# Straight blocks in two stages of a fused 4-layer network: the second routed feed-forward in one block with its routing three groups ahead, and the product-key experts in one block of sixteen steps

## What is computed

```
# second routed feed-forward: one of 8 experts for each batch row
xn = layernorm(h)                                  # [32, 113, 256]
e  = argmax(mean(xn, over the 113 tokens) @ Wr + br)    # one expert number for each row
h += relu(xn[row] @ W1[e] + b1[e]) @ W2[e] + b2[e]      # 256 -> 1024 -> 256

# product-key experts: 8 heads, 8 of 64 x 64 keys for each token and head
xn   = rmsnorm(layernorm(h)) * w
idx  = top 8 of the sums of two top-8 lists of similarities, for each head
h   += sum over the chosen experts of gelu(xn . down[idx]) * relu(score) * up[idx]
```

## Time and profile before

| | us |
|---|---|
| median of 3 runs (lowest to highest) | 6021.89 (6014.45 to 6035.73) |
| the profiled execution, its own time | 6037.05 |
| its span in the trace | 6035.3 |
| second routed feed-forward, first matmul to end of the last residual | 3553.32 to 3911.52 |
| product-key steps, first matmul of the first to last residual | 4631.91 to 6031.2 |

### The profile page before, as it was taken

The page is one execution under the profiler, slowest core; times in us unless marked ns, Lnnn a source line. Parts: engine busy times, 40 slices in busy tenths (PEclk is TensorE's granted clock), DMA queues, the critical chain, the costliest instruction groups (busy, mean ns, idle before and its releaser), DMA issues. The chain is left out here.

```text
span 6035.3 us, 64217 instructions
## 1 busy us (share of the span) xinstructions
PE 4920.7 (82%) x21148; PEld 3219.8 (53%) x21148; DVE 3587.9 (59%) x7080; ACT 2192.0 (36%) x4034; POOL 2261.7 (37%) x1366
## 2 busy tenths in 40 slices
PE   7988699368888878888688767857776999999999
PEld 4555377223333333333244437823335998989998
DVE  3664122269889889898742220055554876867776
ACT  3553011055555545656422232234441222222222
POOL 2442300469999989999700000000001212212211
PEclk8998899589999989899889878978887999999999
DMA  1003133212222222222200006600001000000000
GB/s 66 1 1 108 41 120 99 73 57 71 69 68 69 65 70 69 69 71 69 64 0 5 0 0 237 242 3 0 0 0 74 4 3 4 4 3 4 4 4 4
DMA packets 153762, 289.17 MB, mean 48 GB/s; under 512 B 24373, under 2 KB 135468, under 8 KB 144650
## 3 DMA queue, kind: packets, MB, share of 16 engines
q1 hardware_dynamic: 146426, 267.00, 13.6%
q0 software_dynamic: 6144, 14.04, 0.8%
q10 hardware_dynamic: 912, 4.63, 0.2%
HBM read 254.96 MB, written 33.42 MB: 48 GB/s over the span
## 5 line engine op out<-in xcount | busy, mean ns | idle before, releaser
L1496 PE MATMUL ssm_ps<-ssm_hc,net_ident 128*128 128x452 f32 x2048 | 957.1, 594 | 195.3 <-DVE ssm_hc L1729 111.0
L1659 POOL TENSOR_TENSOR ssm_dBu<-ssm_du,ssm_bc 128x904 f32<-128x904 f32 x512 | 1066.6, 2107 | 14.9 <-DMA ssm_bc<-ssm_rows 12.5
L1585 ACT ACTIVATE ssm_ps<-ssm_step,ssm_decay 128x448 f32<-128x448 f32 x1024 | 649.6, 638 | 665.6 <-DVE ssm_ps L1719 433.8
L1496 PEld LDWEIGHTS ssm_ps<-ssm_hc,net_ident 128*128 128x128 f32 x2048 | 390.4, 203 | 728.9 <-issue 343.1
L2925 POOL TENSOR_TENSOR peer_hot_cols<-peer_hot_cols,peer_codesT 128x512 f32<-128x512 f32 (+1 forms) x240 | 288.5, 1202 | 1159.2 <-DVE peer_hot_cols L2941 1159.2
L1719 DVE TENSOR_TENSOR_SCAN ssm_ps<-ssm_ps,ssm_dBu 128x452 f32<-128x452 f32 x512 | 565.2, 1104 | 128.1 <-ACT ssm_ps L1585 43.8
L1719 DVE TENSOR_TENSOR_SCAN ssm_hs<-ssm_ps,ssm_dBu 128x452 f32<-128x452 f32 x512 | 551.7, 1077 | 62.6 <-ACT ssm_ps L1585 35.8
L1668 POOL TENSOR_TENSOR ssm_hc<-ssm_hs,ssm_bc 128x904 f32<-128x904 f32 x256 | 539.5, 2107 | 74.8 <-DVE ssm_hs L1719 74.6
L2835 PE MATMUL peer_ps<-peer_xn,peer_down 128*128 128x226 f32 x2048 | 451.3, 366 | 24.2 <-issue 17.3
L2938 DVE TENSOR_TENSOR peer_hot_rows<-peer_ramp,peer_codesT 128x1024 f32<-128x1024 f32 (+1 forms) x240 | 284.5, 1186 | 280.0 <-PE peer_ps L2850 249.6
L2850 PEld LDWEIGHTS peer_ps<-peer_hot_cols,peer_hot_rows 128*128 128x128 f32 x3616 | 436.0, 192 | 23.8 <-DVE peer_hot_rows L2938 22.6
(11 more groups left out here) (422 smaller groups left out, 8304.1 us busy)
## 6 DMA issues: line engine op xcount, KB each, us to landing
ssm_bc<-ssm_rows SPq DMA_DIRECT2D x256, 452.0 KB, 3.6
ex_w<-in_l_ffn_w SPq DMA_DIRECT2D x66, 1024.0 KB, 9.4
moe_w_gu<-in_moe_gate_up SPq DMA_DIRECT2D x16, 704.0 KB
slots_in<-rt_zeros SPq DMA_DIRECT2D x17, 640.0 KB, 8.5
moe_rows_in<-slots_in SPq DMA_DIRECT2D x16, 512.0 KB
slots_out<-xp_rows_out SPq DMA_DIRECT2D x16, 512.0 KB
moe_w_dn<-in_moe_down SPq DMA_DIRECT2D x16, 384.0 KB
peer_down<-in_peer_down_t SPq DMA_DIRECT2D x1, 4096.0 KB, 16.4
```

The lines of the kernel that those rows point to most:

```text
L1496: nc.tensor.matmul(Y_BANK[j][:, 0:GT], c["ident"][:, :], hc[:, q % 2, j, :], start=False, stop=(n == S - 1))\
L1585: nc.scalar.activation(rows(dA(i % 2))[:, :, lo:lo + N - 1], rows(step[hf.d][:, j, :])[:, :, lo:lo + N - 1], ACT.Exp, scale=decay[hf.d][:, ...
L1659: nc.gpsimd.tensor_tensor(dBu[:, q % 2, j:j + 2, :], du[hf.d][:, j:j + 2, :], bc[:, q % RING, 0:1, :].to_broadcast([P, 2, GT]), ALU.mult). ...
```

## The change

**Second routed feed-forward.** Everything is one straight block without loops. The norm, the token mean and the router work on one group at a time. Three groups (`AHEAD`) are done first, one after the other; groups 3 to 7 are worked into the expert rows of groups 0 to 4: the mean matmul behind the up matmuls of the group's row 0, the second moment behind those of row 1, the scores behind those of row 3. The normed groups go to four buffers `xs` (`XB`) and the two ScalarE copies are gone. The expert numbers of each group go to DRAM and back by two DMAs of GpSimd's queue. SyncE fetches the expert of row r as soon as row r - 4 is finished. Both halves of the down product share one PSUM bank, and the residual starts when both are done. The semaphores are cleared by GpSimd, as after the first routed feed-forward.

**Product-key experts.** The loop, its three borders and the variant of the step's columns that is taken from registers are gone; all sixteen steps stand in one block.

The core of the diff:

```diff
+    WB = 4
+    XB = 4
+    AHEAD = 3
     with Stage(nc, "ex2") as st:
-        with Stage(nc, "rt2") as sr:
-            with nc.Fori(0, GROUPS // NW) as g:
...
-        with nc.Fori(0, GROUPS) as g:
-            with nc.Block(no_gpsimd_drain=True) as block:
...
-            st.clear()
+        with nc.Block() as block:
+            @block.sync
+            def _(sp):
+                sp.dma_start(w_r[:, :, :], wr.rearrange("(k p) e -> p k e", p=P)).then_inc(s["loaded"], 16)
+                sp.dma_start(b_r[:, :], br.to_broadcast([GB, E])).then_inc(s["loaded"], 16)
+                for r in range(B):
+                    i = r % WB
+                    sp.wait_ge(s["id_in"], 16 * (r // GB + 1))
+                    if r >= WB:
+                        sp.wait_ge(s["down_done"], r - WB + 1)
+                        sp.wait_ge(s["res_done"], DK * (r - WB + 1))
+                    e = nc.sync.value_load(ids[0:1, r:r + 1], min_val=0, max_val=E - 1)
...
+            @block.gpsimd
+            def _(pool):
+                for g in range(GROUPS):
+                    rows = slice(g * GB, (g + 1) * GB)
+                    pool.wait_ge(s["best_done"], g + 1)
+                    nc.gpsimd.dma_start(row_expert[rows, :], best[:, g % 2, 0:1]).then_inc(s["sent"], 16)
+                    pool.wait_ge(s["sent"], 16 * (g + 1))
+                    nc.gpsimd.dma_start(ids[0:1, rows], row_expert[rows, :].rearrange("b a -> a b")).then_inc(s["id_in"], 16)
+                pool.wait_ge(s["id_in"], 16 * GROUPS)
...
+                # TensorE
+                for g in range(AHEAD):
+                    mean(g)
+                    var(g)
+                    scores(g)
+                for r in range(B):
+                    g, i = r // GB + AHEAD, r % GB
+                    up(r)
+                    if g < GROUPS:
+                        if i == 0:
+                            mean(g)
+                        if i == 1:
+                            var(g)
+                        if i == 3:
+                            scores(g)
+                    down(r)
...
+                # ScalarE: squares(g) behind the relus of row 0, roots(g) behind those of row 1
+                # VectorE: centre(g) ahead of the residual of row 1, scale(g) ahead of row 2's,
+                #          choose(g) (bias, maximum, index) behind row 3's
...
+        st.clear(pool_dmas=True)
@@ peer
         LAG = 3
-        U = 4
...
-        with nc.Fori(0, STEPS // U - 1) as g:
-            steps([pair_at(g, k) for k in range(U)], [pair_at(g, k + 1) for k in range(U)], [pair_at(g, k + 2) for k in range(U)])
-        tail = range(STEPS - U, STEPS)
-        steps([pair_cols(g) for g in tail], [pair_cols(g + 1) if g + 1 < STEPS else None for g in tail],
-              [pair_cols(g + 2) if g + 2 < STEPS else None for g in tail])
+        after = lambda g: pair_cols(g) if g < STEPS else None
+        steps([pair_cols(g) for g in range(STEPS)], [after(g + 1) for g in range(STEPS)], [after(g + 2) for g in range(STEPS)])
```

More of the change, by code:

```diff
@@ L2010, in l2_ffn @@
     HB = HID // P
+    WB = 4
+    XB = 4
+    AHEAD = 3
     with Stage(nc, "ex2") as st:
         ps = [st.psum(f"ps{i}") for i in range(8)]
-        normed = st.sbuf("normed", [P, DK, T])
-        means = st.sbuf("means", [P, DK, B])
-        with Stage(nc, "rt2") as sr:
-            NW = 2
-            norms = [Norm(sr, ps[2 * i], ps[2 * i + 1], f"ln{i}") for i in range(NW)]
-            kept, summed = sr.sem("kept"), sr.sem("summed")
-            with nc.Fori(0, GROUPS // NW) as g:
-                with nc.Block(no_gpsimd_drain=True) as block:
[L2021 to L2087, removed]
@@ L2089, in l2_ffn @@
-        WB = GB
+        UP_BANK, DOWN_BANK, LN_BANK = ps[0:4], ps[4:6], ps[6:8]
         W1 = [st.sbuf(f"w1_{i}", [P, DK, HID]) for i in range(WB)]
@@ L2093, in l2_ffn @@
         B2 = [st.sbuf(f"b2_{i}", [P, DK]) for i in range(WB)]
-        ids = st.sbuf("ids", [1, B + 1], U32)
+        w_r = st.sbuf("w_r", [P, DK, E])
+        b_r = st.sbuf("b_r", [GB, E])
+        ids = st.sbuf("ids", [1, B], U32)
         hid = st.sbuf("hid", [P, 2, HB, N])
-        x_in = st.sbuf("x_in", [P, DK, GT])
-        id_in = st.sem("id_in")
-        landed = [st.sem(f"landed{i}") for i in range(WB)]
[L2099 to L2108, removed]
+        xs = st.sbuf("xs", [P, XB, DK, GT])
+        centred = st.sbuf("centred", [P, DK, GT])
+        square = st.sbuf("square", [P, DK, GT])
+        log_var = st.sbuf("log_var", [P, GT])
+        rstd = st.sbuf("rstd", [P, GT])
+        total = st.sbuf("total", [P, DK, GB])
+        means = st.sbuf("means", [P, DK, GB])
+        score = st.sbuf("score", [GB, E])
+        top = st.sbuf("top", [GB, 8])
+        best = st.sbuf("best", [GB, 2, 8], U32)
+        names = ("loaded", "mean_mm", "centre_done", "square_done", "var_mm", "log_done", "rstd_done", "x_done", "total_done",
+                 "mean_done", "score_mm", "score_done", "top_done", "best_done", "sent", "id_in",
+                 "up_done", "relu_done", "down_done", "res_done")
+        s = {x: st.sem(x) for x in names}
+        landed = [st.sem(f"landed{i}") for i in range(WB)]
         with nc.Block() as block:
```

195 lines of the change are left out of this document (133 added, 62 removed).

## The result

| us | before | changed |
|---|---|---|
| median of 4 runs (lowest to highest) | 6025.34 (6014.45 to 6035.73) | 5925.01 (5908.74 to 5927.84) |
| the profiled execution (its span) | 6037.05 (6035.3) | 5927.84 (5926.1) |

The ratio is 0.983, with an interval of 0.980 to 0.985: 100 us less. The two traces differ by 109.2 us. Read at the same places in both, that splits as follows.

The account below looks back on a forecast made before the run. TensorE was taken to bound both stages, with losses at block borders. Experts 69.1 us less plus product keys 32.6 less made 101.7; from the median 6021.9 that gave 5920 us, range 5898 to 5950.

Parts of the forecast that it names:

- Opening: Ahead of the experts: three groups one after the other, 39.8 us at the lower clock, 34.9 at the higher.
- The numbers' way: Expert opening: expert numbers through DRAM and back by 24.3 us at the latest, row 0 loaded by 34.7, hidden before 39.8.
- Rows: Expert stage: 32 rows at 7.14 us, 228.5; cold first row +2.0; five norms of 3.4 between rows, 17.2; stage 288.6.
- The end of the stage: Expert stage's border to the next stage: 1.4 us before; a GpSimd clear may add 0 to 2, taken as 0.5.
- Product keys: Product-key stage: three borders become inner steps, 33.4 us less; 0.8 lost to clock drops, leaving 32.6.
- The clock drops: Product-key inner steps: some take 1.66 us more after a wait for codes; 0.8 for three more steps, range 0 to 20.
- The range's own terms: Whole kernel: opening 34.9 to 44, first row 1 to 3, end 0 to 2, clock drops 0 to 20: 5907 to 5945.
- Weights bind: Rival, expert stage: fetches get only 248 GB/s, 8.5 us a row, 26 us more, 5946; chance 0.08.
- Fresh code binds: Rival, product keys and experts: straight code must be waited for, 52 us less gained, 5972; chance 0.07.
- Slower than before: Rival, expert stage: four-buffer ring with landings of 40 us, kernel ends at 6058; decides from landings of 35; chance 0.03.

Follow-up runs that it names:

- sorted version: Changed kernel with semaphore numbers sorted before clearing, so one range instruction clears neighbours: 5804.62 us, ratio 0.973; the same edit on the kernel before: 5885.29, ratio 0.986.
- `LAG = 4`: Changed kernel with the product keys' routing weights four pieces behind the hidden units instead of three: 5903.94 us.

## Why the prediction was right

5920 was forecast and 5925 measured (5898 to 5950 the range); the ratio, 0.983, is that of the forecast. That the two agree to 5 us is in part luck, since a measurement can tell no less than 18. Read in the traces, the expert stage with its end gave 66.3 us where 69.1 were forecast, and the product keys 31.8 where it was 32.6.

**Opening.** 39.8 by the lower clock, 34.9 by the higher: measured 39.66, with bursts of 3.38 us. The row of another stage was the right neighbour: both are bursts of four with idleness ahead and behind. That the opening runs at the lower clock is shown. The condition that the prediction gives for it, bursts shorter than the waits between them, does not fit this trace: the second burst of each group took 3.38 us behind a wait of 2.18, 2.62 or 2.25, and ran at the lower clock all the same.

**The numbers' way.** At the latest at 24.3, so that row 0 was covered by 5 us. It took 4.9 us from choice (3565.8) to first fetch (3570.67), not up to 10.4: the bound was safe and wide. The Trainium skill's fixed 2.0 us (DMA: Bandwidth & Descriptors, "Anatomy of one DMA — SWDGE (gpsimd) path") puts it at 4 for two transfers, as an estimate, and this trace's first transfer agrees: 1.95 us from its issue to that of the next (3566.12 to 3568.07), and 4.55 from there to the first fetch. Later ones, with the expert fetches beside them, let GpSimd wait 3.5 to 5.8 us. That their way is hidden is shown by the waits: no wait of TensorE on DMA in the stage with three groups ahead, one of 1.0 with two, and 14 us a group with one.

**Rows.** 7.14 for a row and 3.4 for a norm: 28.6 and 31.98 a group, as forecast. The first cold row was +2.9, not +2.0. The whole stage 289.0 against 288.6.

**The end of the stage: the term that was mis-sized.** "A clear on GpSimd may add 0 to 2, I take 0.5." It added 2.9. The gap in the earlier trace rows held 10 clears on SyncE, by the same view of the kernel before:

```profile
L70 SPq EVENT_SEMAPHORE_RANGE_CLEAR  x10: 30/30/35, 3911.9 to 3912.4; - x10
```

I did not ask how many instructions a clear is. Here it is 24 with as many resets, and the sorted version shows that they are the cause: 1.6 instead of 5.0 us. How much of it the resets take was not separated; 24 clears with resets took 3.7 us here, 63 without took as long on SyncE. My first explanation, a drain, was refuted.

**Product keys.** 32.6 forecast, 33.4 measured between the same places. The clock drops cost nothing more, as two came in the kernel before and two now; the prediction counted twelve inner steps there and the trace has eleven intervals, which changes its 0.8 to 0.9. What the first step and the tail lost (1.6) was in no term and no experiment was for it.

**The range's own terms** add up to 5913 to 5946, not 5907 to 5945: opening, first row, end and clock drops can take 7 us from 5920 and add 26. The measured time lies in both.

**Weights bind**: refuted, at one and a half times the traffic too; at twice they do bind. **Fresh code binds**: refuted by the straight steps of 85.57 and the straight groups of 31.98. **Slower than before**: landings of 14.7 us at most, far from 35; but waits for a fetch in every group can cost the whole gain, as one group ahead shows.

**The difference of the traces** is 9 us larger than that of the medians. It lies in RWKV, whose loop takes 72.4 or 75.1 us a round in unchanged code: in the kernel before four of seven rounds were 75.1, in the changed one a single one was over 75. The prediction put the 15 us by which the profiled execution stood above the median outside the change. These rounds fit that, but don't show it. From the first transfer of RWKV to the first similarity matmul the two traces with the old expert stage and single clears take 675.8 and 680.1 us, the nine with the new one 663.4 to 672.6. With the sorted clear it is 640.2 with the old one, 642.8 and 628.1 with the new. So a few of the 100 us may come from what the new stage does to the rounds behind it, or from chance; what sets them was not tried.

## What to carry to other kernels

Ask of every block border what it is made of: here barrier, clears, codes and cold restart were 7.0 to 7.7 us, the loop's jump another 3 to 6, and the semaphore clears of a border up to 4 and together 1% of the kernel, in no engine's busy time. When a routed computation fetches by computed numbers, count how far ahead the numbers are chosen: one group ahead cost 14 us a group, two were enough, and the third cost 9 in a cold opening. For what a stage's new code does first, take the row of a burst with as many matmuls and a like idleness around it, from whatever stage.

## What the runs showed of the hardware that I had not expected

- A semaphore clear is an instruction like others: 0.058 us for each in a border of 63, and 0.067 and 0.075 by the time of the two kernels, by 906 and 1087 of them taken away; a range of many numbers is one. On GpSimd with a reset each, 24 took 3.7 us.
- The clock drops in the product-key steps come at nearly even distances. With one block and the wait of 1.56 us in each step, a step of 87.24 stands at the fourth and eleventh interval of the changed kernel, at the fifth and twelfth with the product keys alone changed, at the third and tenth with two groups ahead. With the sorted clear it is the second, eighth and fifteenth, so the distance isn't always seven. With `LAG = 4`, where the wait is gone, there is none. What sets the distance was not found.
- One core took 415 GB/s from HBM into SBUF for 160 us on end.
- A product-key border with straight code behind it costs nearly the same everywhere (7.0, 7.6 and 7.3 to 7.7 us in the three kernels with single clears, 6.0 with sorted ones), while a jump back costs 3.3 to 6.4 more in what is the same code; why it varies was not tried. For straight code itself no wait was seen, in a block of sixteen steps.
- The kernel before takes 6034 us on one chip (6016.88 to 6037.84) and 5966 on another (5959.6 to 5980.45), which is more than its runs on either differ by.
